# A graph layer's message loop: VectorE waits for a signal of each gather, and does its other work in portions behind each product

## The reference, cut to what matters

```python
x_j = x[src]                                             # 40,000 rows gathered
s_j = silu(x_j[:, 384:] @ W1 + b1) @ W3 + b3             # depends on the node alone
rbf = sqrt(2 / R_CUT) * sin(n * pi * r / R_CUT) / r      # n = 1..20, r: the edge's weight
edge_basis = rbf * cutoff(r) @ W2 + b2                   # 384 numbers per edge
split = s_j * edge_basis                                 # s1, s2, s3
v_msg = v_j * s1[:, :, None] + s3[:, :, None] * edge_attr1[:, None, :]
x = x + segment_sum(concat([v_msg, s2]), dst)            # first sum over edges
# second half, worked out per node: v = v @ U, v_V = v @ V, norm of v_V,
# h = silu([norm, s] @ Wu1 + bu1) @ Wu2 + bu2, v * s1, dot(v, v_V) + s3
x = x + segment_sum(msg2[src], dst)                      # second sum, by edge counts
out = layernorm(x_in + x)
```

## Time and profile before

| | before |
|---|---|
| median of runs | 518.26 us |
| profiled execution, its span | 519.65 us, 517.8 us |
| TensorE busy (matmuls) | 441.8 us, 85% |
| VectorE busy | 427.9 us, 83% |
| ScalarE busy | 357.4 us, 69% |
| GpSimd busy | 353.3 us, 68% |
| mean granted TensorE clock | 0.965 of full |

### The profile page before, as it was taken

How to read it: one execution, slowest core, us unless ns; L and a number is a source line. 1 busy time by engine, 2 the same in 40 slices (tenths; PEclk the granted TensorE clock), 3 DMA queues, 4 the chain that set the end, 5 groups by cost and what they waited for, 6 DMA issues and landing times.

```text
span 517.8 us, 14462 instructions
## 1 busy us (share of the span) xinstructions
PE 441.8 (85%) x5171; PEld 281.2 (54%) x5171; DVE 427.9 (83%) x782; ACT 357.4 (69%) x840; POOL 353.3 (68%) x375
## 2 busy tenths in 40 slices
PE   5948777698897997888988997998898998999995
PEld 3434444355554664554654564565464655678783
DVE  8798978899899899889899989988998987921192
ACT  3549855666866776886797588587685777768452
POOL 8837777777777777777777777777777777740200
PEclk9976999989999999999999999899998999999999
DMA  8897888888988888888888888888888888610022
GB/s 253 285 317 225 259 248 254 265 272 251 277 263 279 252 277 276 258 254 271 259 266 268 274 265 264 264 275 279 248 252 263 277 270 269 203 50 1 3 105 100
DMA packets 46607, 122.86 MB, mean 237 GB/s; under 512 B 9425, under 2 KB 22293, under 8 KB 46525
## 3 DMA queue, kind: packets, MB, share of 16 engines
q0 software_dynamic: 25040, 102.58, 64.3%
q1 hardware_dynamic: 17245, 13.33, 8.1%
q10 hardware_dynamic: 4240, 5.90, 3.3%
HBM read 109.78 MB, written 12.00 MB: 235 GB/s over the span
## 4 chain that ended last, share of the span: by engine, by line
POOL 48%; PE 18%; issue 17%; DMA 8%; DVE 7%; ACT 1%; DVEq 0%; POOLq 0%; SPq 0%; ACTq 0%
POOL side L624 35%; POOL work L624 13%; PE psum L1600 9%; DMA side<-node_table,src_c 4%; DVE side L1166 2%; DMA work<-node_table,src_c 2%; PE psum L1384 2%; DVE side L1163 1%; DMA node_table<-work 1%; PE psum L1491 1%; PE psum L1377 1%; PE psum L1451 1%; DMA work<-in_edge_weight 1%; PE psum L1385 1%; PE psum L1485 1%
## 5 line engine op out<-in xcount | busy, mean ns | idle before, releaser
L624 POOL DMA_INDIRECT side<-node_table,src_c x233 | 235.3, 1010 | 71.0 <-issue 67.6
L1485 PE MATMUL psum<-side,scratch 128*32 128x512 f32 x466 | 126.1, 618 | 0.5 <-DVE side L1166 0.5
L1451 PE MATMUL psum<-w2s,scratch 128*128 128x384 bf16 x313 | 80.1, 339 | 53.8 <-DVE side L1166 46.7
L763 ACT ACTIVATE side<-key_no,less_key 128x140 bf16<-128x140 f32 x313 | 112.5, 413 | 0.4
L1166 DVE TENSOR_TENSOR side<-side,psum 128x768 f32<-128x768 f32 (+1 forms) x117 | 110.4, 943 | 0.0
L1163 DVE TENSOR_TENSOR side<-side,psum 128x512 f32<-128x512 f32 (+1 forms) x117 | 79.6, 681 | 32.0 <-DMA side<-node_table,src_c 31.1
L624 POOL DMA_INDIRECT work<-node_table,src_c x80 | 81.9, 1024 | 31.6 <-issue 30.3
L1491 PE MATMUL psum<-side,scratch 128*32 128x128 f32 x1398 | 100.8, 280 | 0.0
L705 ACT CAST scratch<-psum 128x512 bf16<-128x512 f32 x79 | 46.2, 585 | 66.3 <-PE psum L1444 63.6
L772 ACT ACTIVATE scratch<-side,one_f 128x280 bf16<-128x280 bf16 (+1 forms) x157 | 81.7, 520 | 0.0
L1491 PEld LDWEIGHTS psum<-side,scratch 128*32 128x32 f32 x1398 | 72.4, 111 | 0.4
(11 more groups left out here) (228 smaller groups left out, 754.5 us busy)
## 6 DMA issues: line engine op xcount, KB each, us to landing
side<-node_table,src_c POOLq DMA_INDIRECT x233, 4.4
sum_rows<-stage SPq DMA_DIRECT2D x208, 16.0 KB
sum_rows<-zeros_bf SPq DMA_DIRECT2D x3, 896.0 KB, 6.6
node_table<-work ACTq DMA_DIRECT2D x8, 320.0 KB, 5.4
scratch<-sum_rows SPq DMA_DIRECT2D x10, 256.0 KB, 4.6
out<-xw SPq DMA_DIRECT2D x9, 256.0 KB
xw<-in_x ACTq DMA_DIRECT2D x2, 768.0 KB, 10.8
work<-node_table,src_c POOLq DMA_INDIRECT x80
```

What stands on the lines that cost most here:

```text
L624: g.indirect_dma_start(out=rows[i % SLOT_PAIRS][:, j, :], out_offset=None, in_=node_table, in_offset=bass.IndirectOffsetOnAxis(ap=src_c[:, ...
L763: a.activation(key_off[:, b, j, :], key_no[:, :], ACT.Abs, bias=less_key[:, t:t + 1]).then_inc(L["key_off_made"], 1)
L1451: last = mm(bank[2 * (i % 2) + j][:, 0:C3], stacks[:, (i // 2) % STACK_BUFS, 2 * (i % 2) + j, :], w2s[:, :], start=True, stop=True)
L1485: mm(bank[b][j * SPAN:(j + 1) * SPAN, :], hot[:, n % 2, t + j, 0, :], rows[s][:, j, 0:4 * C], start=first, stop=True, skip_group_check=True)
```

## The change

1. Each gather of the first pass raises a semaphore, `issued`, when GpSimd is through with its instruction (not when the data lands). Of pair i the product of the last columns waits for `issued` >= 2i+6 and that of the vector columns for `issued` >= 2i+7 (LEAD = 4); waits beyond 313 are left out. The waits for the landed data stay.
2. The two products of a pair are no longer neighbours. Behind each stands one portion of the other work: `sender_hots`, `receiver_hots` behind the first, `add_counts` behind the second.
3. Each radial step is cut in two halves of 400 elements, one in the pair's first portion, one in the second. TensorE and ScalarE wait for both halves where they waited for the whole.
4. The steps of the node blocks are cut finer (eight instead of five), and a small planner, `placed`, puts each into the portion with room: 0.93 us behind the first product, 0.70 us behind the second, less what the fixed work takes.
5. The last `add_counts` moves from behind pair 155 to behind pair 156.

```diff
+LEAD = 4
+ROOM = (0.93, 0.70)
...
+        issued = sem("issued")
...
+            for w, f in enumerate(FIRST_SLOT):
+                place("x1_vectors", w, 0.64, [(f, 1), (f, 0)])
+                place("x1_rest", w, 0.21, [(f, 0), (f, 1)])
+                place("residual", w, 0.62, [(f + a, k) for a in (1, 2, 3, 4, 5) for k in (0, 1)])
+                made = place("products", w, 0.48, [(f + a, k) for a in (8, 9) for k in (0, 1)])
...
-            def gather(i):
+            def gather(i, first):
                 if i >= SLOT_PAIRS:
                     pool.wait_ge(L["summed"], i - SLOT_PAIRS + 1)
                 for j in range(tiles_in(i)):
                     g.indirect_dma_start(
                         out=rows[i % SLOT_PAIRS][:, j, :], out_offset=None, in_=node_table,
-                        in_offset=bass.IndirectOffsetOnAxis(ap=src_c[:, 2 * i + j:2 * i + j + 1], axis=0)
+                        in_offset=bass.IndirectOffsetOnAxis(ap=src_c[:, 2 * i + j:2 * i + j + 1], axis=0),
+                        engine_sem=issued if first else None
                     ).then_inc(gathered[i % SLOT_PAIRS], 16)
...
+            def behind_gather(count):
+
+                if count <= NT:
+                    dve.wait_ge(issued, count)
+
+            def rest_messages(i, rows_in):
...
                 dve.wait_ge(L["basis_made"], i + 1)
...
+                if rows_in is None:
+                    behind_gather(2 * i + 2 + LEAD)
...
+            def vector_messages(i, rows_in):
+                if rows_in is None:
+                    behind_gather(2 * i + 3 + LEAD)
...
                 for i in range(PAIRS):
-                    messages(i, rows_in)
                     n = i // GP
+                    rest_messages(i, rows_in)
+                    if i % GP == 1 and n + 1 < LG:
+                        sender_hots(n + 1)
+                    if i % GP == 2 and n + 1 < LG:
+                        receiver_hots(n + 1)
+                    between(i, 0, rows_in is None)
+                    vector_messages(i, rows_in)
...
                     if i % GP == 1 and n >= 1:
                         add_counts(n - 1)
-                    if i == PAIRS - 2:
+                    if i == PAIRS - 1:
                         add_counts(LG - 1)
...
+                    between(i, 1, rows_in is None)
```

More of the change, by code:

```diff
@@ new lines, in high_half, with placed, use, place @@
+        def high_half(p, k, h):
+            halves = cells[:, p % 2].bitcast(BF16).rearrange("p t (e h) -> p t e h", h=2)
+            return halves[:, half_tiles(h), k * N_RBF:(k + 1) * N_RBF, 1]
+        def placed():
+            room = [list(ROOM) for _ in range(PAIRS)]
+            put = {}
+            def use(i, k, us):
+                room[i][k] -= us
+            for i in range(PAIRS):
+                if i % GP == 1:
+                    use(i, 0, 0.5)
+                    if i > GP:
+                        use(i, 1, 0.42)
+                if i % GP == 2:
+                    use(i, 0, 0.59)
+                for k in range(6):
+                    if i in piece_slots(k):
+                        for h in range(2):
+                            use(i, h, 0.31 if k == 1 else 0.5)
+            def place(name, w, us, turns):
+                at = min(turns, key=lambda t: (max(0.0, us - room[t[0]][t[1]]), turns.index(t)))
+                use(*at, us)
+                put.setdefault((name, at[1]), {})[at[0]] = w
+                return at
+            for w, f in enumerate(FIRST_SLOT):
[3 more added lines that the diff above has]
+                made = place("products", w, 0.48, [(f + a, k) for a in (8, 9) for k in (0, 1)])
+                place("dots", w, 0.48, [(f + a, 1) for a in (9, 10, 11) if f + a > made[0]])
+                place("gate_dot", w, 0.21, [(f + a, 0) for a in (13, 14)])
+                place("update_vectors", w, 0.48, [(f + a, 1) for a in (13, 14, 15) if f + a < PAIRS])
+                place("update_rest", w, 0.21, [(f + a, k) for a in (14, 15) for k in (1, 0) if f + a < PAIRS])
+            return put
@@ L632, in _ @@
             for i in range(PAIRS):
-                gather(i)
+                gather(i, True)
             more = passes_needed(pool)
@@ L649, in _ @@
                     for i in range(PAIRS):
-                        gather(i)
+                        gather(i, False)
                 for w in range(NW):
@@ L1044, in less_high, with low_part, both_halves @@
                                 ).then_inc(L["less_high_made"], 1)
-            def low_part(p):
-                dve.wait_ge(L["less_high_made"], p + 1)
-                v.tensor_tensor(piece_cells(p, 0), piece_cells(p, 2), high_half(p, 2), ALU.subtract
+            def low_part(p, h):
+                dve.wait_ge(L["less_high_made"], 2 * p + h + 1)
+                v.tensor_tensor(piece_cells(p, 0, h), piece_cells(p, 2, h), high_half(p, 2, h), ALU.subtract
                                 ).then_inc(L["low_made"], 1)
+            def both_halves(step, p):
+                for h in range(2):
+                    step(p, h)
@@ L1051, in _ @@
             dve.wait_ge(S["harmonic_set"], 1)
-            angles(0)
-            near(0)
-            remainder(0)
+            both_halves(angles, 0)
+            both_halves(near, 0)
+            both_halves(remainder, 0)
             table_vec(0)
@@ L1206, in dots, with gate_of, gate_dot, update_vectors @@
                                 ).then_inc(B["dot_made"], 1)
-            def update(w):
-                dot, first, third = (kept(x1T, w)[:, k * C:(k + 1) * C] for k in range(3))
+            def gate_of(w, k):
+                return kept(x1T, w)[:, k * C:(k + 1) * C]
+            def gate_dot(w):
                 dve.wait_ge(B["gate_taken"], w + 1)
                 dve.wait_ge(B["dot_made"], w + 1)
-                v.tensor_tensor(dot, dot, first, ALU.mult).then_inc(B["dot_scaled"], 1)
+                v.tensor_tensor(gate_of(w, 0), gate_of(w, 0), gate_of(w, 1), ALU.mult).then_inc(B["dot_scaled"], 1)
+            def update_vectors(w):
+                dve.wait_ge(B["gate_taken"], w + 1)
                 dve.wait_ge(B["x1_made"], 2 * w + 2)
@@ L1267, in ending @@
                 dve.wait_ge(L["summed"], PAIRS)
-                def both(step):
+                for steps_of in ((x1_vectors, x1_rest), (residual,), (products,), (dots,), (gate_dot,), (update_vectors, update_rest)):
                     for w in range(EARLY_BLOCKS, NW):
-                        step(w)
-                both(new_x1)
-                both(residual)
-                both(products)
-                both(dots)
-                both(update)
+                        for step in steps_of:
+                            step(w)
                 dve.wait_ge(S["flags_summed"], 1)
```

122 lines of the change are left out of this document (64 added, 58 removed).

## The result

The changed kernel takes 505.39 us (median of four runs, 504.43 to 506.71), the kernel before beside it 517.99 us; the ratio is 0.9762, with a 95% interval of 0.9728 to 0.9797. The forecast was 504.0 in a range of 499 to 513. The medians and ratios of this document leave out the executions that the machine disturbed, of a kernel and of the one before alike.

What follows compares the result with a forecast made beforehand. GpSimd's 313 gathers, one behind the other, were taken as the bound. From the profiled 519.65 us, -14.8 for the stream and +0.6 for the end gave 505.4; from the runs' median 518.26, -14.2 gave 504, range 499 to 513.

Steps and rivals of the forecast that it cites:

- the needy moment: About 0.13 us after a gather's start, when a running VectorE instruction with all operands in SBUF holds it until that ends.
- the row at 315.60: Timeline row before the change: a gather starting under L1151 ends 0.82 us after it, taken as showing that L1151 delays gathers.
- The stream: GpSimd's gathers: of 21.1 us lengthening, 1.3 stay at a set-up instruction and 5 at overfull portions; gain 14.8 us.
- 16 overfull portions: VectorE portions, of 314, longer than their room by 0.01 to 0.30 us; priced at 0.3 us each, 5 us.
- The base: Start of the sum: profiled execution 519.65 us, with the median of the runs 1.4 us below it, 518.26.
- The signal's delay: From a gather's end on GpSimd to VectorE: the signal arrives about 0.06 us later.
- The end: From the last gather to the final matmuls: about 6.0 us to the last product, 9 to the matmuls; together +0.6 us.
- The halves and the waiting: VectorE: halves cost 3 us more, covered by 16 us spare at 1.20 of 1.25 us per gather; waiting costs nothing.
- The first (VectorE becomes the bound): Loop's queue on VectorE, loaded to 96%: waits costing 0.11 us per product give 523 us; chance 0.08 with the third rival.
- the second: Signals late or costly to GpSimd, or portions miss: 509 us if half effective (508 to 513: 0.13), 519 if all lost.
- The third: A gather that starts first holds VectorE's portions, up to 0.5 us in some 250: 600 us; chance 0.08 with the first.

Runs made afterwards that it cites:

- the first kernel with whole steps: The changed kernel with the radial steps undivided, each behind the first product of its pair: 509.72 us, ratio 0.9894.
- the order alone, again: The changed kernel without the waits for the signal, run a second time, beside the changed kernel: 506.29 us, ratio 0.98.
- the products adjacent: The changed kernel without waits for the signal, a pair's two products together again, both portions behind them: 510.2 us, ratio 0.9889.

## Why the prediction was right, and where it wasn't

**The bound, and what lengthens the gathers: right in the main, the needy moment only half.** A held gather ends some 0.82 us after an SBUF-only instruction (L1191, L1153, L1078 above), and none of these is a product. But two conditions were missing. The instruction must have been running when the gather started; one that begins just behind the start holds nothing. And it must read two operands, or be the TENSOR_SCALAR: the TENSOR_REDUCE of the node blocks (L1276, which reads one) runs over the start of the gather at 306.31 in the timeline of the result, and that gather takes 0.94 us. The counts are in the last section. For such instructions the planner's rooms are on the safe side.

The Trainium skill, "SBUF — State Buffer", section "Who interferes with whom", infers that a `tensor_tensor` doesn't hold up descriptor generation, and the prediction set the row at 315.60 against it. That row doesn't refute it. It shows that an indirect gather is held at its start, where it also has row numbers to read from SBUF; further into a gather no `tensor_tensor` holds it (532 cases, last section). What the row rules out is only what the prediction drew from the inference, that L1151 would delay no gather.

**The stream: 14.4 us measured for 14.8.** 6.7 us were left instead of 6.3. The set-up instruction (L1123, now L1172) fell on the fifth gather instead of the fourth, and the first six give 1.5 us where I had 1.3; all others give 5.2 us where I had 5. But those 5.2 us are not quite where I had put them. I priced 16 overfull portions; the trace has 32 gathers over 1.0 us, six of them of the kind at 307.56, where a short mask instruction (L1191) lies on the moment. The number held, the working behind it only roughly, so part of the agreement is luck.

**The base: too high.** 14.4 us came off a trace that had 21.1; the same order on VectorE had 16.8 in the kernel with the unused signal. The medians say 517.99 - 505.39 = 12.6 us, and 515.73 - 504.49 = 11.2 us on another chip, where I forecast 14.2. The step "the median of the runs lies 1.4 us below the profiled execution" carries the whole gain of one execution over to the runs, and that is 1.6 to 3 us too much.

**The signal's delay.** 0.06 us was forecast; it is 0.03 us at the vector product and 0.13 at the product of the last columns, so the first portion has less room than planned. It cost little, as the halves leave room; it cost the kernel with whole steps.

**The end: +1.2 us for +0.6.** The last product ends at 438.28, 6.3 us behind the last gather, forecast 6.0; the first of the final matmuls (L1679, the old L1600) starts at 441.43, 9.4 us behind it, forecast 9. In the timeline, half a microsecond of it:

```profile
434.59 10.02 POOL L681 TENSOR_TENSOR update_low<-scratch,update_high 128x512 fp32r<-128x512 f32 x8 [2.59 <-ACT update_high L873]
...
435.20 0.82 DVE L1296 TENSOR_TENSOR scratch<-work 128x128 f32<-128x128 f32 x1
```

L1296 takes 0.82 instead of 0.29 us, with the last products behind it. I had looked for what VectorE does to GpSimd and not for the reverse.

**The halves and the waiting.** VectorE's load is 1.206 us per gather, as forecast (1.20). TensorE still has room, 48.4 us of waits in the row above where the earlier trace rows has 60.3.

**The rivals.** The first (VectorE becomes the bound) didn't happen: gathers wait for TensorE's sums for 1.8 us only. The signals with the old order do idle VectorE between its products and are 1.45% slower, but there too no gather waited for another engine, so they don't show this rival either. Of the second, the late signal is refuted by the 0.03 and 0.13 us, the sender's cost by the 95.08 us. The third is refuted by the gather's line and by L1200, which runs under gathers with the median that L1151 had:

```profile
L1200 DVE TENSOR_TENSOR scratch<-scratch,slow_c x52: 548/553/737, 41.4 to 426.5; 128x768 bf16<-128x768 f16 x51, 128x896 bf16<-128x896 f16 x1
```

**What was wrong in the reasoning.** I put "the signals and the portions" down as one edit with one price, with the signals as what makes the phase. The runs take it apart: halves (with the finer steps of the node blocks) some 6 us, the products apart some 3 to 5, the signals 1 to 3, no term of which is sharper than that. A kernel without the signals was a rival that I should have priced: it differs from mine by less than 1%.

## What to carry to other kernels

When GpSimd's gathers set the pace, look at which VectorE instruction is running when each gather starts and still runs 0.13 us later: shorten the ones that read two operands in SBUF, and the TENSOR_SCALAR, first, and spread them between those that read PSUM; only then think of a signal. A signal between two engines fixes their phase, so it is only as good as the order that it fixes: with the old order it made this kernel slower. And take the base of a forecast from several traces where a quantity wanders, as the lengthening does here by 4 us between two traces.

## What the hardware showed that I had not expected

**A gather is held at its start, by what is already running.** Two gathers of the changed kernel, each with the same VectorE line running 0.13 us after its start:

```profile
54.08 0.57 DVE L1078 TENSOR_TENSOR scratch<-scratch 128x400 f32<-128x400 f32 x1
...
54.43 1.04 POOL L667 DMA_INDIRECT side<-node_table,src_c  x1 [0.30 <-issue]
...
55.77 0.95 POOL L667 DMA_INDIRECT work<-node_table,src_c  x1 [0.30 <-issue]
55.79 0.58 DVE L1078 TENSOR_TENSOR scratch<-scratch 128x400 f32<-128x400 f32 x1
```

The first L1078 began 0.35 us ahead of its gather, ends at 54.65, and the gather ends 0.82 us later. The second began 0.02 us behind its gather's start, and the gather takes its ordinary 0.95 us. I counted this over the gathers behind the sixth in the 14 traces. Where an SBUF-only TENSOR_TENSOR or TENSOR_SCALAR had begun over 0.05 us ahead of the gather and lasted to 0.19 us into it or longer, the gather was lengthened in all of 578 cases, and in 574 it ended 0.77 to 0.83 us after that instruction. Where it was the TENSOR_REDUCE, none of 44 gathers was lengthened. Where a TENSOR_TENSOR or TENSOR_SCALAR began in the gather's first 0.13 us, 203 of 207 gathers took at most 1.01 us. So the 0.13 us are slack behind the start, not a later moment of need. The gather holds VectorE in turn, but briefly: TENSOR_TENSOR instructions, SBUF-only, that begin from 0.04 us ahead of its start to 0.02 us behind it take up to 0.09 us longer than usual.

Later in a gather the kind of instruction decides. In gathers that nothing held at the start, 532 SBUF-only TENSOR_TENSOR instructions began 0.04 to 0.57 us behind it and ran on to the gather's end or close to it, and no such gather took over 0.98 us. The radial step `near`, a TENSOR_SCALAR, lengthened ten that way, to 0.99 to 1.12 us; in the first kernel with whole steps:

```profile
89.31 1.12 POOL L667 DMA_INDIRECT side<-node_table,src_c  x1 [0.30 <-issue]
89.75 0.57 DVE L1073 TENSOR_SCALAR scratch<-scratch 128x800 f32<-128x800 f32 x1
```

L1073 ends at 90.32, the gather 0.11 us later. Gathers thus have two places where VectorE can hold them, an early one for TENSOR_TENSOR and TENSOR_SCALAR and a late one for the TENSOR_SCALAR alone. That the early one is the reading of the row numbers would fit, but wasn't tried.

**GpSimd's own two-input instructions hold VectorE's.** L681 reads two tiles in SBUF, eight times back to back, each about 1.28 us. A VectorE instruction with both inputs in SBUF that falls among them ends 0.15 us after the end of one of them. In seven traces it got in at the next such end and was 0.69 to 1.12 us long: in the changed kernel L1296 from 435.20 to 436.02, where GpSimd's first ends at 435.87; with the order alone, again, the same piece from 437.76 to 438.45, GpSimd's first ends at 438.30. With the products adjacent it started at 436.17, got in at none of the next five boundaries, and ended 0.15 us after the seventh instruction (443.41 and 443.57), 7.40 us long; GpSimd then stood idle for 0.96 us before its eighth. The products with an operand in PSUM keep their 0.68 and 0.94 us in the same stretches. The Trainium skill, "SBUF — State Buffer", section "Who interferes with whom", says that a VectorE instruction with two SBUF inputs contends with a GpSimd instruction that reads SBUF. By that rule, the trace agrees. That the one that waits can also miss boundary after boundary while GpSimd's queue is full is in the trace only. When it misses them I can't say; it was seen in one execution.

**A signal of a gather's issue** arrives 0.03 us after the end of GpSimd's instruction at an instruction with one wait, 0.13 us at one with three. In front of the second, VectorE's trace has an event instruction of 0.05 us of its own (L1211, the line of the wait for `issued`); ahead of the L1224 at 308.82 it runs from 308.72 to 308.77. Whether it is the number of waits that makes the difference wasn't tried.
